# A recommendation tower on one core: the loops over blocks written out, with constant waits

## The reference

```
e = stack([tbl_f[ids[:, f]] for f in range(26)], axis=1)       # 2048 x 26 x 128
all_emb = concatenate([bottom[:, None, :], e], axis=1)         # 2048 x 27 x 128
gram = einsum('bfd,bgd->bfg', all_emb, all_emb)
z = gram[:, triu_i, triu_j]                                    # 351 pairs a sample
h = concatenate([z, bottom], axis=1)                           # 2048 x 479
h = maximum(h @ W_top1 + b_top1, 0)                            # 512
h = maximum(h @ W_top2 + b_top2, 0)                            # 256
y = h @ W_top3                                                 # 2048 x 1
```

## Time and profile before

| | |
|---|---|
| median of 3 runs | 518.97 us (512.42 to 520.0) |
| the profiled execution | 514.17 us, span 512.4 us |
| PE matmul | 373.3 us, 73% of the span, 5636 instructions |
| PE weight load | 306.9 us, 5636 instructions |
| VectorE | 207.6 us, 41% |
| ScalarE | 166.5 us, 33% |
| GpSimd | 246.8 us, 48% |
| mean granted TensorE clock | 0.877 |

### The profile page before, as it was taken

How to read it: one execution, slowest core, us unless ns; L and a number is a source line. 1 busy time by engine, 2 the same in 40 slices (tenths; PEclk the granted TensorE clock), 3 DMA queues, 4 the chain that set the end, 5 groups by cost and what they waited for, 6 DMA issues and landing times.

```text
span 512.4 us, 13151 instructions
## 1 busy us (share of the span) xinstructions
PE 373.3 (73%) x5636; PEld 306.9 (60%) x5636; DVE 207.6 (41%) x88; ACT 166.5 (33%) x297; POOL 246.8 (48%) x264
## 2 busy tenths in 40 slices
PE   0876824985978776876969759598587858776976
PEld 0866813764757564655757547476466647565774
DVE  5989440540618142360623607054152804032000
ACT  2544150330433216231261314332044312533422
POOL 5573563554635635446344655256454564464010
PEclk9998965896979888798788979699798998897989
DMA  7997121523142411424115321154114241151110
GB/s 193 247 272 204 43 53 29 174 65 117 48 149 72 130 32 47 154 53 136 28 44 170 83 97 44 58 146 139 37 41 157 72 132 28 44 180 50 61 63 12
DMA packets 34111, 50.05 MB, mean 98 GB/s; under 512 B 21252, under 2 KB 23729, under 8 KB 33160
## 3 DMA queue, kind: packets, MB, share of 16 engines
q1 hardware_dynamic: 25214, 32.27, 20.9%
q0 software_dynamic: 8320, 16.86, 12.4%
q10 hardware_dynamic: 522, 0.07, 0.1%
HBM read 38.67 MB, written 10.49 MB: 96 GB/s over the span
## 4 chain that ended last, share of the span: by engine, by line
PE 61%; issue 24%; ACT 5%; DVE 3%; DMA 3%; another core or an unknown queue 2%; SPq 1%; ACTq 1%; DVEq 0%
PE turn_ps L438 26%; PE gram_ps L472 13%; PE mlp_ps L502 8%; PE turn_ps L430 7%; PE mlp_ps L515 4%; DVE onehot L696 3%; DMA work<-tbl 3%; ACT feat L575 2%; PE mlp_ps L486 2%; PE mlp_ps L523 1%; SPq L339 1%; ACTq L284 0%; DVE parts L735 0%; DMA rows<-scratch_last 0%
## 5 line engine op out<-in xcount | busy, mean ns | idle before, releaser
L401 POOL DMA_INDIRECT rows<-tbl,idx x256 | 244.1, 953 | 224.6 <-PE turn_ps L438 92.4
L438 PE MATMUL turn_ps<-onehot,parts 125*128 125x512 f32 (+1 forms) x800 | 178.5, 382 | 33.6 <-issue 24.9
L696 DVE TENSOR_TENSOR onehot<-ids,rows_at 125x4096 fp32r<-125x4096 int32 (+1 forms) x39 | 160.8, 4144 | 64.6 <-issue 22.8
L438 PEld LDWEIGHTS turn_ps<-onehot,parts 125*128 125x128 f32 x800 | 141.0, 209 | 62.4 <-issue 32.4
L472 PE MATMUL gram_ps<-feat 128*27 128x27 f32 x4096 | 66.0, 213 | 72.5 <-issue 65.8
L472 PEld LDWEIGHTS gram_ps<-feat 128*27 128x27 f32 x4096 | 55.3, 126 | 87.2 <-issue 82.2
L729 DVE COPY gram<-gram_ps 128x432 f32<-128x432 f32 x32 | 19.4, 607 | 215.2 <-PE gram_ps L472 215.2
L575 ACT ACTIVATE feat<-turn_ps 128x512 f32<-128x512 f32 (+2 forms) x80 | 76.4, 989 | 82.8 <-PE turn_ps L430 72.1
L430 PE MATMUL turn_ps<-const,rows 128*128 128x128 f32 x272 | 45.4, 294 | 27.5 <-DMA rows<-tbl,idx 13.4
L608 ACT ACTIVATE feat<-turn_ps 128x128 f32<-128x128 f32 x70 | 22.9, 437 | 116.7 <-PE turn_ps L438 37.0
L430 PEld LDWEIGHTS turn_ps<-const,rows 128*128 128x128 f32 x272 | 34.2, 150 | 36.3 <-issue 29.2
(11 more groups left out here) (22 smaller groups left out, 82.8 us busy)
## 6 DMA issues: line engine op xcount, KB each, us to landing
ids<-idx_cols SPq DMA_DIRECT2D x7, 1024.0 KB
scratch<-gram SPq DMA_DIRECT2D x7, 864.0 KB
rows<-tbl,idx POOLq DMA_INDIRECT x256
work<-tbl SPq DMA_DIRECT2D x7, 448.0 KB
scratch<-gram SPq DMA_DIRECT2D x7, 416.0 KB
pairs<-scratch SPq DMA_DIRECT2D x84, 29.2 KB
ids<-idx_cols SPq DMA_DIRECT2D x7, 256.0 KB
third<-tbl SPq DMA_DIRECT2D x3, 448.0 KB
```

What stands on the lines that cost most here:

```text
L401: pool.indirect_dma_start(rows[t][:, j, :], None, tables[TABLE_AT[j - 1]], bass.IndirectOffsetOnAxis(ap=idx[t][:, j - 1:j], axis=0)).then_ ...
L438: pe.matmul(bank, parts[:, x, m, c, :], moving[:, c, :], start=(c == 0 and m == 0), stop=(c == VC - 1 and m == SPLIT - 1)))
L696: dve.tensor_tensor(onehot_of, ids_of.rearrange("p (o n) -> p o n", o=1).to_broadcast((VP, VC, n)), rows_at[0:VP, :].rearrange("p (c o) -> ...
```

## The change

Python writes out the loops of PE, ACT, VectorE and SP, so that the counts are constants. `b` is always a number, and the tests for that go. VectorE's comparisons at the start of a block waited for a group of rows that comes at or behind the last two picks of the block before (`HOT_FREE`), ACT's copy of the staged picks too; now they wait for those picks themselves (`last_pick`).

```diff
-HOT_FREE = [("rows", 0, len(ROWS[0]) - 1), ("rows", 1, 0)]
-STAGED_FULL = HOT_FREE[-1]
...
+def last_pick(b, back=0):
+
+    return group(b, ("pick", SIDE - 1 - back) if b else ("next", len(NEXT) - 1 - back))
...
-            with sp.Fori(1, BLOCKS - 1) as i:
-                block(i)
+            for b in range(1, BLOCKS - 1):
+                block(b)
...
-            with pe.Fori(1, BLOCKS // 2) as i:
+            for i in range(1, BLOCKS // 2):
                 block_steps(2 * i - 1, 1, STEPS)
                 block_steps(2 * i, 0, STEPS)
...
-                act.wait_ge(group_out, group(b - 1, STAGED_FULL) + 1)
+                act.wait_ge(group_out, last_pick(b - 1) + 1)
...
-            with act.Fori(1, BLOCKS // 2) as i:
+            for i in range(1, BLOCKS // 2):
                 for odd in (1, 0):
...
-                    dve.wait_ge(group_done, group(b - 1, HOT_FREE[g]) + 1)
+                    dve.wait_ge(group_done, last_pick(b - 1, HOT - 1 - g) + 1)
...
-            with dve.Fori(1, BLOCKS // 2) as i:
+            for i in range(1, BLOCKS // 2):
                 block_steps(2 * i - 1, 1)
                 block_steps(2 * i, 0)
```

More of the change, by code:

```diff
@@ L109 @@
 LAST_ROWS = [("rows", t, len(ROWS[t]) - 1) for t in range(TB)]
-HOT_FREE = [("rows", 0, len(ROWS[0]) - 1), ("rows", 1, 0)]
-STAGED_FULL = HOT_FREE[-1]
 assert all(GROUP_FIRST[s] <= PRE + GROUP_AT[s] for s in LAST_ROWS)
-assert all(GROUP_FIRST["next", len(NEXT) - HOT + g] <= PRE + GROUP_AT[HOT_FREE[g]] for g in range(HOT))
-assert all(GROUP_AT["pick", SIDE - HOT + g] <= GROUP_AT[HOT_FREE[g]] for g in range(HOT))
 def group(b, step):
-    if isinstance(b, int) and b == 0:
+    if b == 0:
         return GROUP_FIRST[step]
@@ L124, in slot @@
 def slot(b, step):
-    return (GROUP_FIRST if isinstance(b, int) and b == 0 else GROUP_AT)[step] % RING
+    return (GROUP_FIRST if b == 0 else GROUP_AT)[step] % RING
 def feat_end(b, t):
-    if isinstance(b, int) and b == 0 and t == 0:
+    if b == 0 and t == 0:
         return max(group(0, LAST_ROWS[0]), group(0, ("own", len(OWN) - 1))) + 1
     return group(b, LAST_ROWS[t] if t else ("pick", SIDE - 1)) + 1
+def last_pick(b, back=0):
+    return group(b, ("pick", SIDE - 1 - back) if b else ("next", len(NEXT) - 1 - back))
 MLP = 7
@@ L179, in wait @@
 def wait(eng, sem, value):
-    if isinstance(value, int) and value <= 0:
+    if value <= 0:
         return
@@ L293, in load_ids @@
             def load_ids(b):
-                sp.wait_ge(onehot_done, len(OWN) - 1 if isinstance(b, int) else PRE + SIDE * b)
+                sp.wait_ge(onehot_done, len(OWN) - 1 if b == 1 else PRE + SIDE * b)
                 cols = slice(0, (SIDE - 1) * NB2)
@@ L306, in load_tile @@
                 T = TB * b + t
-                if not isinstance(b, int) or b:
+                if b:
                     wait(sp, group_done, group(b - 1, LAST_ROWS[t]) + 1)
@@ L417, in signal @@
             def signal(b, step, n, instruction):
-                if n in (FIRST_SIGNALS if isinstance(b, int) and b == 0 else SIGNALS).get(step, ()):
+                if n in (FIRST_SIGNALS if b == 0 else SIGNALS).get(step, ()):
                     instruction.then_inc(step_done, 1)
```

## The result

| | before | after |
|---|---|---|
| median of the runs made together | 517.25 us (512.42 to 520.0, 4 runs) | 500.78 us (498.17 to 502.94, 4 runs) |
| ratio, 95% interval | | 0.9689 [0.9597, 0.9781] |
| span of the profiled execution | 512.4 us | 498.5 us |

A forecast was written before the change was run, and what follows sets the result against it. PE was taken as the bound (61% of the chain, 24% "issue" idle time). Only PE's two returns counted: 514.17 - 3.4 = 510.8 us, plus 2.4 for half the offset to the median, 513 us; range 501 to 522.

The forecast's parts named there:

- Returns on PE: PE's two loop returns, from last layer to pick 0: written out they save 3.4 us, bounds 1.7 to 9.3.
- Register instructions: 165 on PE in three passes, at most 6.6 us; taken as nothing, being worked off while earlier matmuls run.
- VectorE's and ACT's waits: Earlier counts for a block's first two comparisons and ACT's staged copies: costed at nothing.
- SP: the step that failed: SP's twelve DMAs of pairs are out about 5 us sooner in each of six blocks: costed at nothing.
- The gap before pick 3: Sign in the new profile: PE's gap there stays near 1.5 us; 3 us would speak for slower, denser SP issue.
- time given back in the picks: Rival: PE reaches pick 0 sooner but picks 2 to 4 wait for late counts; nothing won, 517 us, chance 0.13.
- Denser SP: Rival: SP's pauseless issue of pairs delays other engines' counts, 1.83 us more per block in six; 524 us, chance 0.09.
- Reads on the small engines: Rival: written-out ACT and SP each suffer one late instruction read of 3.43 us; 520 us, chance 0.06.
- Nothing comes back: Rival: both idle times at PE's returns and the gaps behind them go, 9.3 us; 507 us, chance 0.2.
- registers too: Rival: PE's register instructions add 6.6 us to 9.3 at the returns, 15.9 us in all; 501 us, chance 0.07.

The follow-up runs named there:

- the second execution: The changed kernel itself, nothing altered, run again on another chip against the kernel before: 501.56 us, ratio 0.9712.

## Why the prediction was wrong in size

**Returns on PE: right in kind, mis-sized.** The forecast had 3.4 us for both. With PE's loop back the sum of the stages is 7.5 us longer, and by the ratios it is 0.9846 against 0.9712 and 0.9689, 1.3 to 1.6% or 7 to 8 us. That lies within the bounds of 1.7 to 9.3. The failed part is the comparison: I took the four starts without a return, 8.94 us in the mean, as what a start would be. But all starts came down: the two former returns by 5.3 us, and the four others by 2.1. So less came back than I had assumed. A start without a return was no fixed measure: its time depends on where the fetched pieces end, and writing the loop out moves that place from block to block. The 32 extra matmuls show the places. 1.7 of the 2.1 us are the one start that lost its idle time ahead of pick 0; the rest is open. The gaps amid the products that I had set against the page of the Trainium skill (Runtime: NRT & Kernel Launch, Instruction fetch mechanics), by which crossings between fetched blocks are mostly hidden, are still there: 1.65 us at 205.80 in the changed kernel, 1.75 us at 171.59 on the third chip. On this the rows were right: among the small products a crossing is often not hidden. But of the two sums drawn from it, 6.4 us if the gaps were to go and 3.4 if they stayed, the measured 7.5 lies nearer to the first, though the gaps themselves did not go.

**Register instructions: nothing, as far as shown.** SP's loop with its counts in registers and constant pairs' addresses lost nothing (0.9636). For PE they were never separated from the returns, so a part of the 7.5 us may be theirs. On SP the registers did cost, but as addresses of DMAs and not as instructions.

**VectorE's and ACT's waits: right.** They are worth nothing, by two runs. Their loops neither.

**SP: the step that failed.** The prediction saw the twelve DMAs get some 5 us shorter and wrote: "The dense layer that wants the pairs comes only behind pick 4 and the products of a tile, by `STEPS`, so I cost this at nothing." This was its costliest sentence. The term measured 10.4 and 10.6 us by the stages and 6 to 10.5 by the ratios, over half of the total. I had asked who reads the pairs, found the dense layer far behind them, and stopped; but the cost lies in work that never reads them, between pick 0 and the end of tile 0's products (233.4 and 232.4 us against 221.5 to 223.4). By which way it gets there is only in part known. The next sentence, that the indices behind the pairs "wait for a count of PE's that comes at about the same time", holds in the kernel before. Against the changed kernel, indices that go out some 5 us later cost about as much in all as SP's loop, half of it in the same stretch. In the kernel before the loss shows in the picks, beside which the pairs go out, and its way there is open.

**The gap before pick 3: wrong.** It was to stay near 1.5 us, and it is 0.68 in block 3 and absent in block 4. The rival of time given back in the picks is refuted for the picks themselves, but right in kind one place later: 12.8 of the 17.9 us come back between pick 4 and the first product, where PE stood still for 3.1 us in block 4 (in the second execution 7.4 of 13.1).

**Denser SP: wrong in sign**, with the pairs at 9.38 us and one gap of over 0.3 us ahead of a pick in six blocks (0.68, in block 3). It had looked at the right place, SP's issue beside the picks; it is the slow issue that goes with the loss. **Reads on the small engines: wrong**, nothing was lost on them: with ACT's and VectorE's loops put back the stages take 339.9 and 342.9 us, with them written out 340.5 and 338.9. (The packets don't tell: they are 44 there too, and 49 with PE's loop.) **Nothing comes back** (507 us) and **registers too** (501 us) came near in microseconds, but both put all of it on PE, and PE's part is 7.5 us of 18.4. That the range nearly took in the result is luck: its low end was the price of a rival, PE's register instructions, that no run bears out.

## What to carry to other kernels

When a queue's DMAs get shorter, don't price them by their reader alone: here twelve DMAs with addresses out of registers took 12.6 to 18.0 us against 9.4, which cost some 10 us of 517 in stages that never read the pairs. Ask what runs beside them and what is queued behind, and on which work the next burst of gathers will fall: small matmuls came in bits under it. A loop's return on PE costs what an undisturbed start would save, and starts that are slow for other reasons understate it. And compare two executions of the same kernel before reading a gain out of one stage: here 5 us moved from one stage to the next with nothing changed.

## What the runs showed of the hardware

Counts of PE's picks reach ACT late on the first chips: before, by 1.2 to 4.5 us in many picks; in the changed kernel mostly at once (0.04 us) for picks 0 to 3, and 2.2 to 4.2 us late for pick 4 (in block 4 ACT's copy is at 290.95, the pick's end at 286.98). Why they are late at all is open. On PE the small products mostly come in bits of 1 to 6 matmuls each 0.7 or 1.4 us while POOL issues a gather every 1.25 us.

PE's stream is fetched in pieces of 256 instructions, and among small products PE stands still for 0.9 to 2.7 us at many of the places where one ends (the 2.7 in the second execution of the changed kernel, at 478.30).

On the third chip the late counts and the bits are not there. The granted clock is 0.97 in the mean against 0.87 (1.00 in the products of tile 0, against 0.57 in the changed kernel on the first chip), every count reaches ACT at once, and the idle time named "issue" before small products shrinks. Waits of PE, changed kernel on the first chip:

```profile
PE gram_ps L473 <- issue: 74.5, 86, 3.2
```

And the kernel with the old waits, on the third:

```profile
PE gram_ps L475 <- issue: 19.3, 17, 2.2
```

The kernel before takes 424 us there and 517 on the others. The gain in per cent is about the same (3.4% by the kernel with the old waits, which the changed kernel equals), but it can't be the same gain, since the products of tile 0 are short there in each kernel. Part of it is the returns, at some 5 us each; the rest on that chip was not taken apart, and the changed kernel itself was not run there. What differs between the chips is open.
